# The head of the last feed-forward stage: attention steps behind each gate half and each up half, instead of in pairs behind both

## Chip, core and metric

One Trainium2 chip, one of its cores. The time of a kernel is device microseconds (us) from start to end of one execution. The kernel before takes 408.97 us as the median of three runs (408.11 to 408.98).

## The reference

Two gated transformer blocks on x of 4 batches x 256 tokens x 256 features. Only the second block matters here: attention with 32 heads of 8 features, then a feed-forward layer with 2:4 sparsity. Each is added to x through a tanh gate.

```python
def _L1_xattn_ref(Q, K, V, attention_mask, w_q, w_k, w_v, w_o, b_o):
    ...
    attn = jax.nn.softmax(scores, axis=-1)
    out = jnp.einsum('bnghm,bmgd->bnghd', attn, v).reshape(B, S, D)
    return out @ w_o.T + b_o

def _L1_ffn_ref(x, w_gate, w_up, w_down):
    ...
    h = jax.nn.silu(jnp.einsum('bsh,hi->bsi', x, w_gate)) * jnp.einsum('bsh,hi->bsi', x, w_up)
    h_sparse = _sparsify_2to4(h)       # of each four neighbours the two largest magnitudes stay
    return jnp.einsum('bsi,ih->bsh', h_sparse, w_down)

x = x + jnp.tanh(g_xattn[1]) * _L1_xattn_ref(_layernorm(x, axis=-1), ctx_2048, ctx_2048, ...)
x = x + jnp.tanh(g_ffn[1]) * _L1_ffn_ref(_layernorm(x, axis=-1), ...)
```

## The kernel before

The program is written out engine by engine; each engine runs its own list in the order in which the Python loops emit it, and semaphores tie the lists together. There is no scheduler. Results of TensorE (PE) go to eight banks. `acquire(pe, stage, i, kind)` takes the next bank of a kind in turn and lets PE wait until the reader of what the bank held last has let go of it (`_taken`). In the last stage the gate and up products use kind "wide", banks 0 to 5; all small transposes use kind "turn1", which is one bank, bank 6; the attention's output projection uses "tok1", bank 7.

The 1024 tokens are 8 tiles of 128; a unit is 4 tiles (512 tokens). When the last batch's attention weights have been multiplied with the values, three things are left, and they are mixed:

- The feed-forward layer. One `gate_up(g, j)` is two products of 128 hidden features x 512 tokens, the gate half "fg" and the up half "fu", each of 2 accumulating matmuls over the 256 features (the trace shows a float32 matmul as two instructions, so 4 for each half and 8 for a `gate_up`). There are 16, i = 0 to 15: g = 0, 1 on tokens 0 to 511, g = 2, 3 on tokens 512 to 1023. ScalarE (ACT) takes fg with a Silu (L930) into one of two silu buffers; VectorE (DVE) multiplies fu by it (L1279) and so frees both. ACT then writes the magnitude (L924); DVE, four products later, decides which two of four stay (`sparsify`, four steps for each g, compares L1240 to L1244 first). After i = 15 PE runs the down products: 8 tiles of 16 matmul instructions each; tiles 0 to 3 need `hs_made` 8 and tiles 4 to 7 `hs_made` 16, which DVE counts in `sparsify`.
- `finish(3, n)`, n = 0 to 11, the last batch's attention output: for each of the two tiles six steps. Steps 0 to 3: PE transposes a quarter of the values ("avT", two instructions, L452, bank 6); DVE divides by the softmax sum in two operations, reciprocal (L1176) and multiply into `att` (L1178), and the second frees the bank. Step 4: PE transposes `att` (L242, bank 6) once all four quarters are there, ACT copies it into `actT` (L892). Step 5: PE multiplies by w_o ("res2", 4 instructions, bank 7) after that copy; DVE adds to x (L985) and takes the statistics for the layer norm (L945, L947); GpSimd (POOL) makes the reciprocal deviation `rstd` (L663, L667).
- The layer norm of the tiles 4 to 7: DVE writes `xn` (L957), PE transposes it (`ln_turn`, L236, bank 6), ACT copies into xT (L746). `LATE_NORM_STEPS` = (3, 4, 6, 7) puts the four PE turns behind the gate_ups 3, 4, 6 and 7, and DVE's norms behind its multiplies 2, 3, 5 and 6. The first product on tokens 512 to 1023 (gate_up 8) waits for all eight turns.

The head is the loop over n = 0 to 7 below in PE's list: `gate_up(n)`, then `finish(3, 2n)` and `finish(3, 2n+1)` for n up to 5, then a `ln_turn` where there is one. ACT and DVE walk their own loops over the same i in the same pattern.

Of the kernel before, what the change touches and what calls it, by code (L numbers as in the profile page):

```python
# [7 lines left out]
P = 128  # L8
BATCH, SEQ, DIM = 4, 256, 256
TOKENS = BATCH * SEQ  # L10
TILES = TOKENS // P
KT = DIM // P
# [28 lines left out]
def build_program(nc, a, out):  # L41
# [6 lines left out]
    with ctx:  # L48
        def sb(name, shape, dt=F32):
            return ctx.enter_context(nc.sbuf_tensor(name, shape, dt))  # L50
# [3 lines left out]
        def sem(name):  # L54
            if name not in sems:
                sems[name] = ctx.enter_context(nc.semaphore(name))
            return sems[name]
# [16 lines left out]
        f_gate = f_flat[:, 0:KT * FFN_I].rearrange("p (t n) -> p t n", t=KT)  # L74
        f_up = f_flat[:, KT * FFN_I:2 * KT * FFN_I].rearrange("p (t n) -> p t n", t=KT)
# [22 lines left out]
        xT = sb("xT", [P, KT, TOKENS])  # L98
# [82 lines left out]
        def acquire(pe, stage, i, kind):  # L181

            n = turns.get(kind, 0)
            turns[kind] = n + 1
            bank = KINDS[kind][n % len(KINDS[kind])]
            if bank in occupant:
                before, m = occupant[bank]
                pe.wait_ge(sem(before + "_taken"), m + 1)
            occupant[bank] = (stage, i)
            fills[stage, i] = banks[bank][:, :]  # L190
            return fills[stage, i]

        def filled(eng, stage, i):

            eng.wait_ge(sem(stage + "_ready"), i + 1)
            return fills[stage, i]

        def ready(ins, stage):
            ins.then_inc(sem(stage + "_ready"), 1)

        def taken(ins, stage):
            ins.then_inc(sem(stage + "_taken"), 1)
# [11 lines left out]
        def tile_cols(k):  # L214
            return slice(k * P, (k + 1) * P)
# [11 lines left out]
        def _(pe):  # L227
            def mm(dst, lhsT, rhs, first, last):
                return pe.matmul(dst, lhsT, rhs, start=first, stop=last)  # L229

            def ln_turn(layer, k, kind="turn"):
                dst = acquire(pe, f"ln{layer}", k, kind)
                pe.wait_ge(sem(f"xn{layer}"), k + 1)
                src = xn1[:, HALF_ORDER[k], :] if layer == 1 else xn[:, k % 2, :]
                for t in range(KT):
                    ins = pe.transpose(dst[:, tile_cols(t)], src[:, tile_cols(t)], ident[:, :])  # L236
                ready(ins, f"ln{layer}")

            def turn_pair(stage, i, src, kind):
                dst = acquire(pe, stage, i, kind)  # L240
                for t in range(KT):
                    ins = pe.transpose(dst[:, tile_cols(t)], src[:, tile_cols(t)], ident[:, :])  # L242
                ready(ins, stage)
# [6 lines left out]
            for i in range(4):  # L250
                h, u = divmod(i, UNITS)
                dst = acquire(pe, "rq", i, "main")
                pe.wait_ge(sem("ln0_taken"), UNIT_TILES * (u + 1))
                ready(mm(dst, wh[:, h, :], xT[:, h, u * UNIT:(u + 1) * UNIT], True, True), "rq")
            for i in range(4):
# [3 lines left out]
                dst = acquire(pe, "rk", i, "main")  # L259
                ready(mm(dst, wh[:, h, :], ctxT[:, h, u * UNIT:(u + 1) * UNIT], True, True), "rk")  # L260

            for h in range(RET_HEADS):
                dst = acquire(pe, "rs", h, "main")
                pe.wait_ge(sem("rk_taken"), 2 * h + 2)
                for t in range(2):
                    for b in range(BATCH):
                        at = b * SEQ + t * P
                        ins = mm(dst[:, 2 * P * t:2 * P * t + SEQ - t * P], kT0[:, h, at:at + P],
                                 qT0[:, h, at:(b + 1) * SEQ], b == 0, b == BATCH - 1)
                ready(ins, "rs")  # L270

            for k in range(TILES):
                dst = acquire(pe, "rv", k, "main")
                for h in range(RET_HEADS):
                    ins = mm(dst[:, h * P:(h + 1) * P], ctxT[:, h, tile_cols(k)], wh[:, h, :], True, True)
# [10 lines left out]
            for i in range(4):  # L286
# [3 lines left out]
                dst = acquire(pe, "ro", i, "main")  # L290
                pe.wait_ge(sem("a_made"), 2 * h + 2)
                for t in range(2):
                    ins = mm(dst, amat[:, h, t * SEQ + st * P:t * SEQ + st * P + P], v0[:, t, h, :], t == 0, t == 1)
# [40 lines left out]
            dst = acquire(pe, "rank", 0, "main")[:, 0:(TILES + 1) * EXPERTS].rearrange("p (k e) -> p k e", e=EXPERTS)  # L334
            pe.matmul(dst[:, 0:TILES, :], tri[:, 0, :], onehot16[:, :, :], start=True, stop=False, skip_group_check=True)
            for k in range(TILES):
                later = TILES - k
                ins = pe.matmul(dst[:, k + 1:TILES + 1, :], tri[:, 1, :],
                                onehot16[:, k, :].unsqueeze(1).to_broadcast([P, later, EXPERTS]),
                                start=False, stop=(k == TILES - 1), skip_group_check=True)  # L340
# [101 lines left out]
            def finish(b, n):  # L442

                nt, c = divmod(n, 6)
                i = 2 * b + nt
                if c < PER_GROUP:
                    f = 4 * i + c
                    dst = acquire(pe, "avT", f, "turn1")
                    if c == 0:
                        pe.wait_ge(sem("av_taken"), 4 * b + 2 + nt + 1)  # L450
                    for q in range(HALVES):
                        ins = pe.transpose(dst[:, tile_cols(q)], avT[nt][:, q, c * P:(c + 1) * P], ident[:, :])  # L452
                    ready(ins, "avT")
                elif c == PER_GROUP:
                    pe.wait_ge(sem("avT_taken"), 4 * i + 4)
                    turn_pair("atT", i, att[:, i % 2, :], "turn1")
                else:
                    dst = acquire(pe, "res2", i, "tok1")[:, 0:DIM]
                    pe.wait_ge(sem("atT_taken"), i + 1)
                    for t in range(KT):  # L460
                        ins = mm(dst, actT[:, i % 2, t, :], wo1[:, t, :], t == 0, t == KT - 1)
                    ready(ins, "res2")
# [81 lines left out]
                            scores(b + 2, n)  # L544


            def gate_up(g, j):
                u, blk = divmod(g, FFN_BLOCKS)
                us = slice(u * UNIT, (u + 1) * UNIT)
                c = j * 2 * P + blk * P  # L550
                for stage, w in (("fg", f_gate), ("fu", f_up)):
                    dst = acquire(pe, stage, 4 * g + j, "wide")
                    for t in range(KT):
                        ins = mm(dst, w[:, t, c:c + P], xT[:, t, us], t == 0, t == KT - 1)
                    ready(ins, stage)

            def down(k, kind):
                u, c = k // UNIT_TILES, (k % UNIT_TILES) * P
# [5 lines left out]
            pe.wait_ge(sem("ln3_taken"), UNIT_TILES)  # L564
            loaded(pe, "f", 3)
            for n in range(8):
                gate_up(n // 4, n % 4)
                for c in range(2 * n, min(2 * n + 2, 12)):
                    finish(BATCH - 1, c)
                if n in LATE_NORM_STEPS:  # L570
                    ln_turn(3, UNIT_TILES + LATE_NORM_STEPS.index(n), "turn1")
            pe.wait_ge(sem("ln3_taken"), TILES)
            for j in range(4):
                gate_up(2, j)
            for j in range(4):
                gate_up(3, j)
# [363 lines left out]
        def _(dve):  # L940
# [225 lines left out]
            def finish(b, n):  # L1166
                nt, c = divmod(n, 6)
                i = 2 * b + nt
                if c == 0 and i >= 2:
                    dve.wait_ge(sem("atT_ready"), i - 1)  # L1170
                if c < PER_GROUP:

                    o = att[:, i % 2, :].rearrange("p (q j h d) -> p h q j d", q=HALVES, j=QUADS, h=PER_GROUP)
                    f = 4 * i + c
                    src = filled(dve, "avT", f)[:, 0:2 * P].rearrange("p (q j r) -> p q j r", q=HALVES, j=QUADS)
                    dve.reciprocal(rden[:, f % 2, :, :], src[:, :, :, HD]).then_inc(sem("rden_made"), 1)  # L1176
                    dve.wait_ge(sem("rden_made"), f + 1)
                    taken(dve.tensor_tensor(out=o[:, c, :, :, :], in0=src[:, :, :, 0:HD],  # L1178
                                            in1=rden[:, f % 2, :, :].unsqueeze(3).to_broadcast([P, HALVES, QUADS, HD]),
                                            op=ALU.mult), "avT")  # L1180
                elif c > PER_GROUP:
                    dve.wait_ge(sem("bias_added"), i + 1)
                    residual("res2", i, 1)
                    dve.wait_ge(sem("res2_taken"), i + 1)
                    stat(3, i, x_sb[:, i, :])
# [87 lines left out]
            for g in range(FFN_BLOCKS * UNITS):  # L1273
                for j in range(4):
                    i = 4 * g + j
                    u, blk = divmod(g, FFN_BLOCKS)
                    src = filled(dve, "fu", i)
                    dve.wait_ge(sem("fg_taken"), i + 1)
                    taken(dve.tensor_tensor(out=hs[u][:, 4 * blk + j, :], in0=src, in1=silu[:, i % 2, :], op=ALU.mult), "fu")  # L1279
                    for c in range(2 * i, min(2 * i + 2, 12)):  # L1280
                        finish(BATCH - 1, c)
                    if i + 1 in LATE_NORM_STEPS:
                        norm(3, UNIT_TILES + LATE_NORM_STEPS.index(i + 1))
                    if g >= 1:
                        sparsify(g - 1, j)
# [101 lines left out]
```

## Time and profile before

| | |
|---|---|
| median of three runs | 408.97 us |
| the profiled execution's own time | 409.77 us |
| its span | 407.7 us |
| PE busy in the span | 343.9 us (84%) |
| DVE, ACT, POOL busy | 214.6, 160.1, 98.2 us |
| head of the last stage (gate_up 0 to 7) | 308.9 to 349.7 us |
| gate_up 8 to 15, then the down products | 349.7 to 405.1 us |

An engine's busy time is the sum of its instructions; matmuls are pipelined, so their lengths overlap and the distance between starts says more than a length does. The idle time in brackets behind an instruction group of the timeline is what the engine stood still ahead of it, with the instruction that released it.

### The profile page before, as it was taken

How to read it: one execution, taken by the hardware profiler on the slowest of the kernel's cores; microseconds unless marked ns; L12 is line 12 of the kernel's file. 1: busy time of each engine (PE TensorE's matmuls, PEld its weight loads, DVE VectorE, ACT ScalarE, POOL GpSimd, SP SyncE). 2: the span in 40 equal slices, each digit the busy share in tenths (PEclk: the TensorE clock that was granted, in tenths of full speed). 3: DMA queues.
4: the chain of work that ended last, by engine and by line, in shares of the span. 5: the costliest groups of instructions: out<-in, count | busy, mean ns of one | idle time of the engine just before them, and what ended most of it. 6: DMA issues, size and time to landing. Idle time of an engine off the chain costs nothing.

```text
span 407.7 us, 4563 instructions
## 1 busy us (share of the span) xinstructions
PE 343.9 (84%) x1477; PEld 206.9 (51%) x1477; DVE 214.6 (53%) x509; ACT 160.1 (39%) x336; POOL 98.2 (24%) x148
## 2 busy tenths in 40 slices
PE   2999785519999848989799989979889879999997
PEld 1485564406665526545454555444443434444886
DVE  5134985601232248879446934881241338679921
ACT  2443221204333123145873875477873223333000
POOL 7102543430000346301340442054450001000000
PEclk9999998558999656999999999998999999999999
DMA  7995000143111115400000000000000000000011
GB/s 214 382 424 110 1 13 2 45 151 115 54 39 53 39 47 172 195 6 0 9 0 2 0 6 2 0 2 8 0 2 0 0 2 0 0 0 2 13 51 39
DMA packets 13879, 22.40 MB, mean 55 GB/s; under 512 B 2033, under 2 KB 11249, under 8 KB 13042
## 3 DMA queue, kind: packets, MB, share of 16 engines
q1 hardware_dynamic: 13090, 20.03, 14.4%
q0 software_dynamic: 768, 2.10, 1.6%
q8 instruction: 12, 0.20, 0.2%
q14 instruction: 9, 0.07, 0.1%
HBM read 15.83 MB, written 6.03 MB: 54 GB/s over the span
## 4 chain that ended last, share of the span: by engine, by line
PE 58%; DVE 19%; ACT 8%; issue 7%; POOL 4%; DMA 3%; SPq 0%; DVEq 0%; ACTq 0%; POOLq 0%
PE bank L229 43%; DVE mx L1150 8%; PE bank L438 5%; ACT region L874 5%; PE bank L406 3%; DVE stats L945 2%; POOL x_sorted L691 2%; PE bank L409 2%; PE bank L242 1%; POOL rstd L667 1%; DVE x_sb L985 1%; ACT qst L825 1%; PE bank L452 1%; DMA x_sb<-in_x_dram 1%; PE bank L486 1%
## 5 line engine op out<-in xcount | busy, mean ns | idle before, releaser
L1150 DVE TENSOR_REDUCE mx<-bank 128x2 f32<-128x512 f32 (+1 forms) x96 | 59.8, 684 | 14.0 <-PE bank L409 14.0
L874 ACT ACTIVATE region<-bank,padcol 128x512 f32<-128x512 f32 x96 | 60.8, 701 | 12.6 <-PE bank L229 11.6
L729 POOL TENSOR_SCALAR_AFFINE_SELECT region<-region 128x1024 f32<-128x1024 f32 x32 | 35.0, 1094 | 94.6 <-ACT region L874 94.3
L229 PE MATMUL bank<-xT,e_gu 128*128 128x512 f32 x128 | 56.6, 594 | 0.5 <-ACT xT L746 0.5
L229 PE MATMUL bank<-qst,kblk 128*128 128x512 f32 x96 | 46.1, 507 | 1.6 <-ACT region L874 0.7
L406 PE MATMUL bank<-kblk,qst 128*128 128x512 f32 x96 | 43.3, 475 | 1.6 <-DVE mx L1150 0.9
L229 PEld LDWEIGHTS bank<-xT,e_gu 128*128 128x128 f32 x128 | 23.8, 190 | 28.0 <-issue 27.1
L663 POOL TENSOR_SCALAR veps<-mv 128x1 f32<-128x1 f32 x40 | 11.3, 283 | 80.5 <-DVE mv L947 80.1
L409 PE MATMUL bank<-causb,identb 128*128 128x256 bf16 (+1 forms) x96 | 30.6, 319 | 0.0
L746 ACT ACTIVATE xT<-bank 128x256 f32<-128x256 f32 x32 | 12.4, 386 | 44.1 <-PE bank L236 43.9
L229 PE MATMUL bank<-e_down,region 128*128 128x256 f32 x128 | 27.8, 379 | 0.0
L985 DVE SCALAR_TENSOR_TENSOR x_sb<-bank,tg,x_sb 128x256 f32<-128x256 f32 x24 | 11.6, 482 | 29.2 <-PE bank L229 28.9
L236 PE MATMUL bank<-ident,xn 128*128 128x128 f32 x48 | 12.2, 350 | 17.2 <-DVE xn L957 15.2
L229 PEld LDWEIGHTS bank<-e_down,region 128*128 128x128 f32 x128 | 24.3, 190 | 3.7 <-issue 0.5
L406 PEld LDWEIGHTS bank<-kblk,qst 128*128 128x128 f32 x96 | 18.3, 190 | 13.2 <-DVE mx L1150 9.3
L667 POOL TENSOR_TENSOR rstd<-veps,power 128x1 f32<-128x1 f32 x40 | 24.2, 604 | 3.3
L1122 DVE TENSOR_TENSOR sact<-bank,silu 128x176 f32<-128x176 f32 x15 | 5.1, 342 | 37.6 <-ACT silu L840 37.6
L1279 DVE TENSOR_TENSOR region<-bank,silu 128x512 f32<-128x512 f32 x16 | 11.0, 690 | 26.0 <-PE bank L229 26.0
L229 PEld LDWEIGHTS bank<-qst,kblk 128*128 128x128 f32 x96 | 18.7, 201 | 9.1 <-ACT region L874 7.3
L930 ACT ACTIVATE silu<-bank 128x512 f32<-128x512 f32 x16 | 9.6, 597 | 33.5 <-PE bank L229 33.5
L438 PE MATMUL bank<-region,vaug 128*32 128x512 f32 x192 | 22.7, 597 | 0.0
L229 PE MATMUL bank<-e_gu,sT 128*128 x60 | 21.8, 488 | 0.3 <-ACT sT L834 0.3
(155 smaller groups left out, 557.0 us busy)
## 6 DMA issues: line engine op xcount, KB each, us to landing
e_gu<-in_e_gu_dram SPq DMA_DIRECT2D x2, 1408.0 KB, 12.6
x_sorted<-zero SPq DMA_DIRECT2D x1, 1920.0 KB, 10.3
y_sorted<-region SPq DMA_DIRECT2D x15, 128.0 KB, 1.7
x_sb<-in_x_dram SPq DMA_DIRECT2D x4, 256.0 KB, 4.0
ctxT<-in_ctxT_dram SPq DMA_DIRECT2D x2, 512.0 KB, 7.6
e_down<-in_e_down_dram SPq DMA_DIRECT2D x1, 1024.0 KB, 13.6
region<-x_sorted SPq DMA_DIRECT2D x1, 1024.0 KB, 7.4
e_gu<-in_f_gate_dram SPq DMA_DIRECT2D x1, 1024.0 KB, 4.8
```

Of the source, the lines that this page charges most:

```text
L229: return pe.matmul(dst, lhsT, rhs, start=first, stop=last)
L236: ins = pe.transpose(dst[:, tile_cols(t)], src[:, tile_cols(t)], ident[:, :])
L406: pe.matmul(dst, qst[:, s, q, hg, tile_cols(nt)], kblk[s][q][:, quads, 0:(nt + 1) * P], start=True, stop=False, skip_group_check=True)
L409: ready(pe.matmul(diagonal, identb[:, :], causb[:, 0:diagonal.shape[1], :], start=False, stop=True, skip_group_check=True), "sa")
L438: ins = pe.matmul(dst[32 * j:32 * j + 32, :], vaug[:, 2 * b + mt, 4 * q + j, :], rhs, start=(mt == 0), stop=(mt == nt), skip_group_check=True)
L663: pool.tensor_scalar(veps[:, layer, k:k + 1], mv[:, layer, k, 1:2], eps, None, ALU.add)\
L667: pool.tensor_tensor(out=rstd[:, layer, k:k + 1], in0=veps[:, layer, k:k + 1], in1=power[:, :], op=ALU.pow).then_inc(sem(f"rstd{layer}"), 1)
L729: pool.affine_select(out=block, in_=block, compare_op=ALU.is_ge, fill=0.0, base=0, pattern=[[0, 2], [0, PER_GROUP], [1, P]], channel_multi ...
L746: taken(act.activation(xT[:, :, tile_cols(tile)], src[:, 0:DIM].rearrange("p (t n) -> p t n", t=KT), ACT.Copy), f"ln{layer}")
L874: taken(act.activation(dst, src.rearrange("p (h n) -> p h n", n=SEQ - mt * P), ACT.Exp, bias=padcol[:, key:key + 1], scale=float(HD) ** -0 ...
L985: dve.scalar_tensor_tensor(out=x_sb[:, tile, :], in0=filled(dve, stage, k)[:, 0:DIM], scalar=tg[:, g:g + 1], in1=x_sb[:, tile, :], op0=ALU ...
L1150: taken(dve.reduce_max(mx[:, b % 2, nt, quads, q, hg], src, AX), "sa")
```

## The change

The halves become a function of their own, `half_piece`. In PE's list `finish(3, 2n)` now stands between the gate half and the up half, and `finish(3, 2n+1)` behind the up half. In DVE's list `finish(3, 2i)` moves ahead of the multiply of fu, `finish(3, 2i+1)` stays behind it. The lists of ACT, POOL and SyncE, and the order in which banks are acquired within each kind, stay as they were. No instruction is added or removed.

```diff
@@ -544,15 +544,18 @@
                             scores(b + 2, n)
 
 
-            def gate_up(g, j):
+            def half_piece(stage, w, g, j):
                 u, blk = divmod(g, FFN_BLOCKS)
                 us = slice(u * UNIT, (u + 1) * UNIT)
                 c = j * 2 * P + blk * P
-                for stage, w in (("fg", f_gate), ("fu", f_up)):
-                    dst = acquire(pe, stage, 4 * g + j, "wide")
-                    for t in range(KT):
-                        ins = mm(dst, w[:, t, c:c + P], xT[:, t, us], t == 0, t == KT - 1)
-                    ready(ins, stage)
+                dst = acquire(pe, stage, 4 * g + j, "wide")
+                for t in range(KT):
+                    ins = mm(dst, w[:, t, c:c + P], xT[:, t, us], t == 0, t == KT - 1)
+                ready(ins, stage)
+
+            def gate_up(g, j):
+                half_piece("fg", f_gate, g, j)
+                half_piece("fu", f_up, g, j)
 
             def down(k, kind):
                 u, c = k // UNIT_TILES, (k % UNIT_TILES) * P
@@ -564,9 +567,12 @@
             pe.wait_ge(sem("ln3_taken"), UNIT_TILES)
             loaded(pe, "f", 3)
             for n in range(8):
-                gate_up(n // 4, n % 4)
-                for c in range(2 * n, min(2 * n + 2, 12)):
-                    finish(BATCH - 1, c)
+                half_piece("fg", f_gate, n // 4, n % 4)
+                if 2 * n < 12:
+                    finish(BATCH - 1, 2 * n)
+                half_piece("fu", f_up, n // 4, n % 4)
+                if 2 * n < 12:
+                    finish(BATCH - 1, 2 * n + 1)
                 if n in LATE_NORM_STEPS:
                     ln_turn(3, UNIT_TILES + LATE_NORM_STEPS.index(n), "turn1")
             pe.wait_ge(sem("ln3_taken"), TILES)
@@ -1274,11 +1280,13 @@
                 for j in range(4):
                     i = 4 * g + j
                     u, blk = divmod(g, FFN_BLOCKS)
+                    if 2 * i < 12:
+                        finish(BATCH - 1, 2 * i)
                     src = filled(dve, "fu", i)
                     dve.wait_ge(sem("fg_taken"), i + 1)
                     taken(dve.tensor_tensor(out=hs[u][:, 4 * blk + j, :], in0=src, in1=silu[:, i % 2, :], op=ALU.mult), "fu")
-                    for c in range(2 * i, min(2 * i + 2, 12)):
-                        finish(BATCH - 1, c)
+                    if 2 * i < 12:
+                        finish(BATCH - 1, 2 * i + 1)
                     if i + 1 in LATE_NORM_STEPS:
                         norm(3, UNIT_TILES + LATE_NORM_STEPS.index(i + 1))
                     if g >= 1:
```

PE's list from the head's first gate half on, before (a number behind "bank" is the bank; L229 are products, with `xT,e_gu` the gate and up halves in turn and `wo1,actT` the output projection, L452 the quarter transposes, L242 the `att` transpose):

```order
L229 MATMUL bank2<-xT,e_gu 128x512 x2
L229 MATMUL bank3<-xT,e_gu 128x512 x2
L452 MATMUL bank6<-ident,prod 128x128 x4
L229 MATMUL bank4<-xT,e_gu 128x512 x2
L229 MATMUL bank5<-xT,e_gu 128x512 x2
L452 MATMUL bank6<-ident,prod 128x128 x4
L229 MATMUL bank0<-xT,e_gu 128x512 x2
L229 MATMUL bank1<-xT,e_gu 128x512 x2
L242 MATMUL bank6<-ident,att 128x128 x2
L229 MATMUL bank7<-wo1,actT 128x256 x2
```

The same place now:

```order
L229 MATMUL bank2<-xT,e_gu 128x512 x2
L452 MATMUL bank6<-ident,prod 128x128 x2
L229 MATMUL bank3<-xT,e_gu 128x512 x2
L452 MATMUL bank6<-ident,prod 128x128 x2
L229 MATMUL bank4<-xT,e_gu 128x512 x2
L452 MATMUL bank6<-ident,prod 128x128 x2
L229 MATMUL bank5<-xT,e_gu 128x512 x2
L452 MATMUL bank6<-ident,prod 128x128 x2
L229 MATMUL bank0<-xT,e_gu 128x512 x2
L242 MATMUL bank6<-ident,att 128x128 x2
L229 MATMUL bank1<-xT,e_gu 128x512 x2
L229 MATMUL bank7<-wo1,actT 128x256 x2
```

Two fills of bank 6 that stood back to back (x4) now have half a gate_up between them, and so have the `att` transpose and the projection that needs it. At n = 3 and 4 a layer-norm transpose follows. Before:

```order
L229 MATMUL bank2<-xT,e_gu 128x512 x2
L229 MATMUL bank3<-xT,e_gu 128x512 x2
L452 MATMUL bank6<-ident,amat 128x128 x4
L236 MATMUL bank6<-ident,xn 128x128 x2
L229 MATMUL bank4<-xT,e_gu 128x512 x2
```

And now:

```order
L229 MATMUL bank2<-xT,e_gu 128x512 x2
L452 MATMUL bank6<-ident,amat 128x128 x2
L229 MATMUL bank3<-xT,e_gu 128x512 x2
L452 MATMUL bank6<-ident,amat 128x128 x2
L236 MATMUL bank6<-ident,xn 128x128 x2
L229 MATMUL bank4<-xT,e_gu 128x512 x2
```

Of three fills of bank 6 in a row, two are left in a row. DVE's list for n = 0, before (L1279 is the multiply of fu, of bank 3 here):

```order
L1279 TENSOR_TENSOR region<-bank3,silu 128x512
L1176 RECIPROCAL rden<-bank6 128x8
L1178 TENSOR_TENSOR att<-bank6,rden 128x8x8
L1176 RECIPROCAL rden<-bank6 128x8
L1178 TENSOR_TENSOR att<-bank6,rden 128x8x8
```

And now (the lines are those of the changed file, six or eight higher):

```order
L1182 RECIPROCAL rden<-bank6 128x8
L1184 TENSOR_TENSOR att<-bank6,rden 128x8x8
L1287 TENSOR_TENSOR region<-bank3,silu 128x512
L1182 RECIPROCAL rden<-bank6 128x8
L1184 TENSOR_TENSOR att<-bank6,rden 128x8x8
```

The first of the two quarter steps has moved ahead of the multiply; the second stands behind it as before.

## Rows read from the trace of the kernel before

**Rows 1.** The page: the span, PE and its granted clock in 40 slices.

```profile
span 407.7 us, 4563 instructions
...
PE   2999785519999848989799989979889879999997
...
PEclk9999998558999656999999999998999999999999
```

**Rows 2.** Stretches: busy time (instructions) of PE, PEld, DVE, ACT, POOL; PEclk.

```profile
308.90:349.70 40.80, 34.34 (x104) 16.35 (x100) 19.25 (x47) 12.10 (x23) 2.04 (x4) 1.00 0.00 0
349.70:405.00 55.30, 55.28 (x192) 36.41 (x192) 35.24 (x60) 10.04 (x18) 0.00 (x0) 1.00 0.05 17
```

**Rows 3.** The chain of waits, 309 to 350 us: start, length, what.

```profile
312.66 0.24 DVE region L1279
...
313.27 0.21 DVE rden L1176
...
313.50 0.24 DVE att L1178
...
313.78 0.44 PE bank L452 x2
...
322.94 0.39 ACT actT L892
...
323.46 4.55 PE bank L229 x12
```

**Rows 4.** Timeline of PE through the head: start, length, what, idle before.

```profile
308.92 3.70 PE L229 MATMUL bank<-xT,e_gu 128*128 128x512 f32 x8
312.46 0.38 PE L452 MATMUL bank<-ident,prod 128*128 128x128 f32 x2
313.78 0.44 PE L452 MATMUL bank<-ident,prod 128*128 128x128 f32 x2 [0.94 <-DVE att L1178]
314.05 3.60 PE L229 MATMUL bank<-xT,e_gu 128*128 128x512 f32 x8
...
319.08 3.60 PE L229 MATMUL bank<-xT,e_gu 128*128 128x512 f32 x8
...
324.40 3.60 PE L229 MATMUL bank<-xT,e_gu 128*128 128x512 f32 x8
...
330.43 3.60 PE L229 MATMUL bank<-xT,e_gu 128*128 128x512 f32 x8
...
336.45 3.60 PE L229 MATMUL bank<-xT,e_gu 128*128 128x512 f32 x8
...
341.77 3.60 PE L229 MATMUL bank<-xT,e_gu 128*128 128x512 f32 x8
...
345.43 3.60 PE L229 MATMUL bank<-xT,e_gu 128*128 128x512 f32 x8
...
349.71 2.84 PE L229 MATMUL bank<-xT,e_gu 128*128 128x512 f32 x6 [0.47 <-ACT xT L746]
```

**Rows 5.** The page: the Silu of the gate halves.

```profile
L930 ACT ACTIVATE silu<-bank 128x512 f32<-128x512 f32 x16 | 9.6, 597 | 33.5 <-PE bank L229 33.5
```

**Rows 6.** Timeline of DVE: compare, multiply 5, two norms, last sparsify step.

```profile
337.59 1.76 DVE L1240 TENSOR_TENSOR ctxT<-region 128x1536 bf16<-128x1536 f32 x1 [1.46 <-ACT region L924]
...
341.00 0.69 DVE L1279 TENSOR_TENSOR region<-bank,silu 128x512 f32<-128x512 f32 x1
...
343.12 0.40 DVE L957 TENSOR_SCALAR xn<-x_sb,mv,rstd 128x256 f32<-128x256 f32 x1
...
346.77 0.41 DVE L957 TENSOR_SCALAR xn<-x_sb,mv,rstd 128x256 f32<-128x256 f32 x1
...
388.25 1.28 DVE L1270 SCALAR_TENSOR_TENSOR region<-amat,region 128x512 f32<-128x512 bf16 x2
```

**Rows 7.** Line 667 from 300 to 350 us: shortest, median, longest ns; starts.

```profile
L667 POOL TENSOR_TENSOR rstd<-veps,power x4: 567/570/863, 305.1 to 343.7; 128x1 f32<-128x1 f32 x4
```

**Rows 8.** Stretches, as rows 2: one with a lower granted clock.

```profile
132.50:142.70 10.20, 8.78 (x28) 5.50 (x26) 2.46 (x5) 1.58 (x7) 3.33 (x4) 0.68 0.11 39
```

## The prediction

> **What bounds the kernel now.** I read the page first, then the stretches, then the chain of waits and PE's timeline in the head. The page shows PE busy in nearly every slice of the second half, at full granted clock from slice 32 on [rows 1]. The two stretches separate the last stage: from 349.7 us to the end PE is busy 55.28 of 55.30 us, so nothing but PE's own work counts there; in the head it is busy 34.34 of 40.80 us, at a granted clock of 1.00, which is its upper level, 2.4 GHz [rows 2]. Whatever PE stands still in the head is therefore paid in full at the end, and the head is the place to price. DVE is busy 19.25 us and ACT 12.10 us of it: neither is short of time, PE waits for single operations of theirs.
>
> The chain shows which. At the end of gate_up 0 PE has put the first quarter into bank 6 and needs the same bank for the second. DVE holds it up with three operations in a row: the multiply of fu from 312.66, the reciprocal at 313.27, the multiply into `att` at 313.50, and PE goes on at 313.78 [rows 3]. From 312.46 to 313.78 is 1.32 us for one fill and one release [rows 4]. The other kind of wait is that of the projection for ACT's copy of the `att` transpose (322.94, and PE on at 323.46) [rows 3].
>
> **Sizing the waits.** I take the price of PE's pure work from the tail, where it never waits: 55.28 us for 64 instructions of 512 columns and 128 of 256, which is 0.432 us for one of 512 and 0.216 for one of 256 [rows 2]. A gate_up is 8 x 0.432 = 3.46 us, a half 1.73, a projection 4 x 0.216 = 0.86. gate_up 6 with one transpose pair and no wait takes 345.43 - 341.77 = 3.66 us [rows 4], so a pair costs 0.20. Now each step of the head, start to next start [rows 4], less its pure work:
>
> - n = 0: 314.05 - 308.92 = 5.13, less 3.46 and 2 pairs = 1.27 (0.10 of it is start-up: 308.92 to 312.46 is 3.54 where others take about 3.44)
> - n = 1: 5.03 - 3.86 = 1.17
> - n = 2: 5.32 - 3.46 - 0.20 - 0.86 = 0.80
> - n = 3: 6.03 - 3.46 - 3 pairs = 1.97
> - n = 4: 6.02 - 4.06 = 1.96
> - n = 5: 5.32 - 4.52 = 0.80
>
> Together 7.97 us. Ahead of gate_up 8 there is one more wait, 0.47 us for ACT's copy into xT [rows 4].
>
> **What the change does to each.** Two uses of bank 6 within a gate_up are now a pair and a half apart, 0.20 + 1.73 = 1.93 us, where the worst release in the trace, the one with a multiply of fu ahead of it, takes 1.32. The release of the first step no longer has the multiply in front, that of the second still has, and behind it PE has the next gate half to run: 0.6 us to spare in both. So the 1.17 of n = 0 and of n = 1 go.
>
> At n = 2 and 5 the projection now comes 1.93 us after the start of the `att` transpose, where it came 0.94 after it, waiting. But the gate half's Silu is now ready with the transpose and stands ahead of the copy in ACT's list: 0.60 us [rows 5], which puts the projection at 0.94 + 0.60 = 1.54 at worst. 0.4 us to spare: both 0.80 go. The cover is the up half; without it the price would be 0.80 + 0.60 each.
>
> At n = 3 and 4 three uses of bank 6 become two in a row, `finish(2n+1)` and the layer-norm transpose. DVE's release of the last quarter still has the multiply of fu ahead, so this wait is the 1.17 of n = 1; what goes is 1.97 - 1.17 = 0.80 and 1.96 - 1.17 = 0.79. Its next fill of bank 6 comes a gate half after ACT's copy began, so nothing is left over from there.
>
> Sum of what goes: 1.17 + 1.17 + 0.80 + 0.80 + 0.79 + 0.80 = 5.53 us. No instruction is added. PE's switch between shapes costs nothing new: n = 6 has the same products and a pair at 3.66 us [rows 4].
>
> **What is late next.** DVE has the same work in less time, so I carried its list through. By the steps above gate_up 5 starts about 4.65 us earlier than its 336.45 (n = 0, 1 and 2, 3, 4: 1.17 + 1.17 + 0.80 + 0.80 + 0.79 = 4.73, less rounding): 331.8. The compares began 1.14 us after that start and the multiply 5 behind them 4.55 after it [rows 6]; they hang on that layer-norm turn and ACT, so they move with it: multiply 5 at 336.35. The norms of tiles 6 and 7 follow it by 2.12 and 5.77 us [rows 6]: 338.5 and 342.1, done 0.4 later. PE reaches the turns at 331.8 + 1.73 + 0.20 + 1.73 + 0.86 + 3.46 = 339.8 and, with 0.20 + 3.46 more, 343.4. Both norms are there 0.9 us before. The wait ahead of gate_up 8 stays as it is. In the tail `hs_made` 16 is complete at 389.53 [rows 6] and needed when the last 64 of PE's instructions begin, about 405.1 - 64 x 0.216 = 391.3: 1.7 us to spare, and DVE's last multiply hangs on PE, so both move together.
>
> One rule bears on the norm of tile 7, which needs `rstd` from POOL. The row: L667 takes 0.57 us but once 0.86, the last, begun at 343.7, while DVE runs `sparsify` operations with two inputs in SBUF [rows 7]. The Trainium skill, "SBUF — State Buffer", section "Who interferes with whom", says that a VectorE instruction with two SBUF inputs and a GpSimd instruction that reads SBUF exclude each other for a whole instruction. The trace agrees as far as 0.29 us goes. By the row `rstd` is ready 2 us before the norm. By the rule at its harshest POOL would come on only behind all seven `sparsify` operations and the norm would start some tenths late, still inside the 0.9; it adds nothing to the sum and a little to rival 2.
>
> **The number.** 409.77 - 5.53 = 404.24 us for the profiled execution. That execution lies 0.80 above the median of the three runs, 408.97, so I expect a median of 403.5 us, a gain of 1.35%. Bounds of the uncertain terms: what is left at n = 3 and 4 may be 1.1 to 1.3 each, the spare 0.4 to 0.9 us may be used up once, and the median of before may itself be off by 0.5: 402.7 to 404.6 for the likeliest case.
>
> **Rivals.**
>
> 1. *The projection's wait stays.* ACT's copy stands behind a Silu that now becomes ready at the same moment. For it: the order in ACT's list is unchanged. Against it: 0.4 us to spare by the rows. If the two projection waits stay at 0.80 the gain is 3.9 us: 405.1 us. Chance 0.07.
> 2. *DVE becomes the late one.* Multiply 5 stands behind 3.4 us of compares, and the norms of tiles 6 and 7 behind it. If that chain came 2 us later than I have it, 1.1 us would be lost at the two last turns: 404.6 us. Were DVE's tail chain not to move at all with PE, only its 1.7 us spare would remain as gain: 407.3 us. For it: DVE is the busiest reader (35.24 of 55.30 us in the tail); against it: it idles in between. Chance 0.07, nearly all at the first price.
> 3. *The granted clock falls in the head (slower).* The finer mix of transposes and products, or another alignment, leaves part of the head at the lower level, 1.2 GHz. The trace has a stretch with PE busy 8.78 of 10.2 us at a mean grant of only 0.68 [rows 8]. The head's 32.2 us of pure work (40.80 - 7.97 - about 0.6) at 0.68 would cost 32.2 x (1/0.68 - 1) = 15.2 us: 418.7 us. It decides from a mean grant of 0.85 down, where 32.2 x (1/0.85 - 1) = 5.7 eats the gain. Against it: the head had 1.00 with more standing still than now, and the tail has 1.00 with none [rows 2]. Chance 0.02.
> 4. *It does not do what it says:* some wait I don't see stands in front of each half, for instance for a gate or up bank that is given back late, and the wait only moves. The six banks of that kind are acquired in the same order, three gate_ups apart, and no such wait shows now. 408 to 409 us. Chance 0.04.
>
> The forecast has 0.80. What a measurement of this kernel can tell from no change is about 0.2%, 0.8 us. Slower by more than that: rival 3 and half a hundredth or so of the unforeseen, 0.03. Within it: most of rival 4, 0.03. Faster: 0.94. The range, 402.6 to 405.4, takes in the likeliest case with rival 1 and the first price of rival 2.
>
> **What would show it.** In the changed profile: the L452 pairs with no idle before them; the projection with none; two idles of about 0.94 us ahead of L236 (behind the `att` multiply, 1.3 us after the pair before), and the 0.47 ahead of gate_up 8. gate_up 0 to 7 should last about 35.3 us where they lasted 40.8, and the tail still 55.3. Wrong would be: idle ahead of L452 pairs or the projection (1), ahead of the last two L236 (2), a PEclk under 1.00 in the head (3), idle ahead of gate or up halves (4).

## The result and the profile after

| | before | changed |
|---|---|---|
| median of 6 runs, us | 409.15 (408.11 to 410.38) | 403.04 (402.38 to 405.15) |
| profiled execution's own time, us | 409.77 | 402.70 |
| span, us | 407.7 | 400.6 |
| head (first gate half to gate_up 8), us | 40.79 | 35.33 |

The ratio is 0.9858, with a 95% interval from 0.9832 to 0.9884: a gain of 1.2 to 1.7%, where 1.35% was forecast. The median forecast was 403.5 us, the measured one is 403.04. One of the six changed executions, the one of 405.15 us, had a mean granted clock of 0.928 over its span where the other five had 0.936; it was not profiled, so no row shows in which stage its clock was lower.

PE's timeline of the changed kernel through the head (start, length, what, and in brackets the idle time ahead; the products are still L229, the turns L236) answers [rows 4]:

```profile
307.26 1.98 PE L229 MATMUL bank<-xT,e_gu 128*128 128x512 f32 x4
309.08 0.38 PE L452 MATMUL bank<-ident,prod 128*128 128x128 f32 x2
309.30 1.88 PE L229 MATMUL bank<-xT,e_gu 128*128 128x512 f32 x4
311.02 0.38 PE L452 MATMUL bank<-ident,prod 128*128 128x128 f32 x2
311.24 1.88 PE L229 MATMUL bank<-xT,e_gu 128*128 128x512 f32 x4
...
316.83 0.38 PE L242 MATMUL bank<-ident,att 128*128 128x128 f32 x2
...
318.77 1.03 PE L229 MATMUL bank<-wo,actT 128*128 128x256 f32 x4
...
323.29 0.38 PE L452 MATMUL bank<-ident,amat 128*128 128x128 f32 x2
324.61 0.44 PE L236 MATMUL bank<-ident,xn 128*128 128x128 f32 x2 [0.94 <-DVE att L1184]
324.88 1.88 PE L229 MATMUL bank<-xT,e_gu 128*128 128x512 f32 x4
...
329.86 0.44 PE L236 MATMUL bank<-ident,xn 128*128 128x128 f32 x2 [0.94 <-DVE att L1184]
330.13 1.88 PE L229 MATMUL bank<-xT,e_gu 128*128 128x512 f32 x4
...
338.08 0.38 PE L236 MATMUL bank<-ident,xn 128*128 128x128 f32 x2
...
341.74 0.38 PE L236 MATMUL bank<-ident,xn 128*128 128x128 f32 x2
342.59 9.71 PE L229 MATMUL bank<-xT,e_gu 128*128 128x512 f32 x22 [0.47 <-ACT xT L752]
```

No idle stands ahead of any L452 pair or of the projection at 318.77; the two idles of 0.94 ahead of the layer-norm turns of n = 3 and 4 and the 0.47 ahead of gate_up 8 are all that is left. 342.59 - 307.26 = 35.33 us. The two stretches, in the columns of [rows 2]:

```profile
307.26:342.59 35.33, 32.99 (x104) 16.17 (x100) 19.15 (x47) 11.90 (x23) 2.04 (x4) 1.00 0.00 0
342.59:398.00 55.41, 55.36 (x192) 36.40 (x192) 35.20 (x61) 10.03 (x18) 0.00 (x0) 1.00 0.05 17
```

The head keeps its granted clock of 1.00, and PE still doesn't wait in the tail. From gate_up 8 to the end of the span it is 58.0 us in both kernels (407.7 - 349.71 and 400.6 - 342.59): nothing is given back.

The two spans differ by 7.1 us and the heads by 5.46 only. The other 1.66 us lie ahead of the head, which begins at 308.92 before and at 307.26 now. That is not the change: in the ten profiled executions of this text the head begins between 306.77 and 309.36, and all their kernels have the same lists up to there. The length of the head is therefore what the experiments below are read by; it was the same to 0.01 us in both profiled executions of pe_only below.

### The profile page after: what moved, and what is told of

Same layout as the page of the kernel before. It is cut to its first block, busy times and chain, and to the rows that moved or that the text cites. A ratio compares the mean times of both kernels' runs of the same rounds, so it can differ in the third digit from the quotient of the medians.

```text
span 400.6 us, 4557 instructions
## 1 busy us (share of the span) xinstructions
PE 340.5 (85%) x1471; PEld 205.7 (51%) x1477; DVE 214.3 (54%) x509; ACT 160.0 (40%) x336; POOL 98.4 (25%) x148
## 3 DMA queue, kind: packets, MB, share of 16 engines
HBM read 15.83 MB, written 6.03 MB: 55 GB/s over the span
## 4 chain that ended last, share of the span: by engine, by line
PE 57%; DVE 20%; ACT 8%; issue 7%; POOL 4%; DMA 3%; another core or an unknown queue 1%; SPq 0%; DVEq 0%; ACTq 0%; POOLq 0%
PE bank L229 43%; DVE mx L1156 9%; ACT region L880 5%; PE bank L438 5%; PE bank L406 3%; DVE stats L951 2%; POOL x_sorted L697 2%; POOL rstd L673 2%; PE bank L242 1%; DVE x_sb L991 1%; PE bank L409 1%; DMA x_sb<-in_x_dram 1%; PE bank L452 1%; PE bank L486 1%; PE bank L236 1%
## 5 line engine op out<-in xcount | busy, mean ns | idle before, releaser
L229 PE MATMUL bank<-xT,e_gu 128*128 128x512 f32 x128 | 57.6, 594 | 0.5 <-ACT xT L752 0.5
L229 PE MATMUL bank<-qst,kblk 128*128 128x512 f32 x96 | 46.0, 506 | 1.6 <-ACT region L880 0.7
L229 PEld LDWEIGHTS bank<-xT,e_gu 128*128 128x128 f32 x128 | 23.3, 190 | 25.1 <-issue 24.3
L409 PE MATMUL bank<-causb,identb 128*128 128x256 bf16 (+1 forms) x90 | 28.3, 314 | 0.0
L229 PE MATMUL bank<-e_down,region 128*128 128x256 f32 x128 | 27.8, 379 | 0.0
L236 PE MATMUL bank<-ident,xn 128*128 128x128 f32 x48 | 12.2, 349 | 18.2 <-DVE xn L963 15.5
L991 DVE SCALAR_TENSOR_TENSOR x_sb<-bank,tg,x_sb 128x256 f32<-128x256 f32 x24 | 11.5, 480 | 27.8 <-PE bank L229 27.5
L229 PEld LDWEIGHTS bank<-e_down,region 128*128 128x128 f32 x128 | 24.3, 190 | 3.7 <-issue 0.5
L229 PEld LDWEIGHTS bank<-qst,kblk 128*128 128x128 f32 x96 | 18.8, 202 | 9.0 <-ACT region L880 7.2
L229 PE MATMUL bank<-e_gu,sT 128*128 x60 | 21.6, 484 | 0.3 <-ACT sT L840 0.3
L229 PE MATMUL bank<-e_down,sT 128*128 (+1 forms) x60 | 19.6, 426 | 1.4 <-ACT sT L861 1.4
```

Of the source, the lines that this page charges most:

```text
L409: ready(pe.matmul(diagonal, identb[:, :], causb[:, 0:diagonal.shape[1], :], start=False, stop=True, skip_group_check=True), "sa")
L991: dve.scalar_tensor_tensor(out=x_sb[:, tile, :], in0=filled(dve, stage, k)[:, 0:DIM], scalar=tg[:, g:g + 1], in1=x_sb[:, tile, :], op0=ALU ...
```

## The experiments

Each is a small change of the kernel before or of the changed kernel; turn_mid and norm_early build on ln_bank7. "Head" is, in each trace, from the first gate half to the first half of gate_up 8. The medians are of 4 to 10 executions (pe_only_again: one), the ratios against executions of the kernel before run alongside, whose medians were 409.36 us for pe_only, dve_only, two_banks and ln_bank7, 409.69 us for copy_late, turn_mid, norm_early and pe_only_again, and 409.15 us for the changed kernel.

| kernel | head, us | median, us | ratio (95%) |
|---|---|---|---|
| before | 40.79 | 409.15 | |
| changed | 35.33 | 403.04 | 0.9858 (0.9832 to 0.9884) |
| pe_only | 41.77 | 410.17 | 1.0013 (0.9998 to 1.0028) |
| pe_only_again | 41.77 | 411.20 | |
| dve_only | 39.42 | 408.04 | 0.9965 (0.9945 to 0.9985) |
| two_banks | 36.49 | 404.85 | 0.9890 (0.9866 to 0.9913) |
| copy_late | 35.33 | 403.71 | 0.9852 (0.9833 to 0.9871) |
| ln_bank7 | 33.02 | 402.24 | 0.9807 (0.9783 to 0.9832) |
| turn_mid | 32.96 | 401.79 | 0.9810 (0.9795 to 0.9825) |
| norm_early | 32.40 | 401.26 | 0.9794 (0.9779 to 0.9810) |

**Only PE's list (pe_only).** The changed kernel with DVE's list put back:

```diff
-                    if 2 * i < 12:
-                        finish(BATCH - 1, 2 * i)
                     src = filled(dve, "fu", i)
...
-                    if 2 * i < 12:
-                        finish(BATCH - 1, 2 * i + 1)
+                    for c in range(2 * i, min(2 * i + 2, 12)):
+                        finish(BATCH - 1, c)
```

> PE's list as in the changed kernel (halves apart), DVE's list as before (both steps of finish behind the multiply of fu). My theory: at n = 0, 1, 3, 4 PE's wait is for DVE's release of bank 6 behind the multiply, so splitting PE's list alone only moves it from in front of the second pair's old place to its new one: it stays at about 1.1 us each at n = 0 and 1, and two waits each at n = 3 and 4; only the two projection waits at n = 2 and 5 (0.80 each) go. Head 40.8 - 1.6 = 39.2 us, about 407.5 us in all. Rival (distance alone does it: half a gate_up between two fills of bank 6 hides the release wherever DVE has the multiply): head near the 35.3 us of the changed kernel, about 403 us.

Measured: no gain; the head is 0.98 us longer. PE's timeline:

```profile
310.15 1.88 PE L229 MATMUL bank<-xT,e_gu 128*128 128x512 f32 x4
313.19 0.44 PE L452 MATMUL bank<-ident,prod 128*128 128x128 f32 x2 [1.16 <-DVE att L1184]
...
322.37 1.03 PE L229 MATMUL bank<-wo,actT 128*128 128x256 f32 x4
...
329.20 0.64 PE L236 MATMUL bank<-ident,xn 128*128 128x128 f32 x2 [0.56 <-DVE att L1184]
329.64 3.41 PE L229 MATMUL bank<-xT,e_gu 128*128 128x512 f32 x4
332.89 0.38 PE L452 MATMUL bank<-ident,amat 128*128 128x128 f32 x2
```

And DVE's, at n = 0:

```profile
312.07 0.69 DVE L1285 TENSOR_TENSOR region<-bank,silu 128x512 f32<-128x512 f32 x1 [7.91 <-PE bank L229]
312.68 0.20 DVE L1182 RECIPROCAL rden<-bank 128x8 f32<-128x8 f32 x1
```

The rival is out: distance alone does not help. The first quarter is in bank 6 early, but DVE comes to it only behind the multiply, which waits for the up half; so the second quarter still waits for multiply, reciprocal and multiply into `att`, 1.16 us of idle against 0.94 before. From the up half's end to the second quarter it is 1.32 us in both kernels; before, the first pair's 0.22 us lay inside that time, now they are paid besides it. The projection waits are gone, as expected. Step by step, from PE's starts, the head of pe_only lasts 5.36, 5.25, 4.52, 6.40, 7.77 and 4.52 us for n = 0 to 5, against 5.13, 5.03, 5.32, 6.03, 6.02 and 5.32 [rows 4]. So my 39.2 us was wrong twice. The waits behind the multiply are about 0.22 us longer each, 0.88 in all. And at n = 4 there is something new, the gate half that starts at 329.64 and takes 3.25 us where others take 1.72. The stretches, in the columns of [rows 2]:

```profile
323.20:328.20 5.00, 3.85 (x11) 1.51 (x10) 2.50 (x8) 0.60 (x1) 0.87 (x2) 1.00 0.00 0
328.20:329.60 1.40, 0.83 (x4) 0.60 (x5) 0.75 (x3) 0.00 (x0) 0.00 (x0) 0.89 0.00 0
329.60:332.90 3.30, 3.30 (x7) 1.28 (x6) 0.00 (x0) 0.90 (x2) 0.00 (x0) 0.53 0.00 0
```

The granted clock was 0.53 in this stretch, in effect its lower level of 1.2 GHz (finer stretches have 0.50 from 329.3 to 332.5 us). Ahead of it PE had waited 1.16 us, turned one pair, waited 0.56 more and begun the next pair. The layer-norm turn ahead of the gate half is slow too, 0.44 us from start to start where it is 0.27 otherwise, so the lower clock costs 1.53 + 0.17 = 1.70 us. That is rival 3 of the prediction, in the wrong kernel. To see whether it was chance I ran the same kernel once more.

> The kernel of pe_only once more, to see whether the lower granted clock (0.53 from 329.6 to 332.9 us, behind waits of 1.16 and 0.56 us) comes again. If it belongs to this order of waits: the gate half after the layer-norm turn of n = 3 or 4 takes about 3.3 us instead of 1.7 again, head 41 to 42 us. If it was a chance of that execution: head 40.2 us (the step lengths of pe_only without the 1.53 us of the slow half).

It came again in nearly the same place, and the head lasted 41.77 us again; the one execution took 411.20 us. Its stretches:

```profile
325.00:330.00 5.00, 3.71 (x12) 1.40 (x10) 2.26 (x8) 0.60 (x1) 0.87 (x2) 1.00 0.00 0
330.00:335.00 5.00, 4.58 (x10) 2.33 (x11) 0.66 (x3) 1.50 (x3) 0.00 (x0) 0.66 0.02 3
```

Here the gate half takes 3.01 us, and the pair and the up half behind it lose 0.20 each: 1.7 us again. So in both profiled executions the lower clock came at n = 4 and cost 1.7 us. The other executions were not profiled; their mean granted clocks fit it, 0.929 or 0.933 in all eleven executions of this kernel against 0.933 or 0.937 in the 31 of the kernel before run alongside (3.3 us at 0.53 lower a mean over 408 us by 0.004). Without the lower clock the head would be 41.77 - 1.70 = 40.07 us, 0.72 under before: 1.60 less for the projections, 0.88 more for the bank.

**Only DVE's list (dve_only).** The kernel before with `finish(3, 2i)` ahead of DVE's multiply:

```diff
+                    if 2 * i < 12:
+                        finish(BATCH - 1, 2 * i)
                     src = filled(dve, "fu", i)
...
-                    for c in range(2 * i, min(2 * i + 2, 12)):
-                        finish(BATCH - 1, c)
+                    if 2 * i < 12:
+                        finish(BATCH - 1, 2 * i + 1)
```

> DVE's list as in the changed kernel (first step of finish ahead of the multiply of fu), PE's list as before (both steps behind both halves). My theory: the wait between the two pairs falls from 1.32 to about 0.99 us start to start (a release without the multiply in front), 0.33 us less at each of n = 0, 1, 3, 4; at n = 3 and 4 the layer-norm turn then meets the multiply and gives 0.33 or more back; n = 2 and 5 unchanged. Head about 40.0 us (39.5 to 40.8), in all 408.0 to 409. Rival (DVE's order is what mattered): more than 2 us gained.

Measured: head 39.42, 1.37 us shorter. PE and DVE at n = 3:

```profile
325.07 0.38 PE L452 MATMUL bank<-ident,amat 128*128 128x128 f32 x2
326.08 0.44 PE L452 MATMUL bank<-ident,amat 128*128 128x128 f32 x2 [0.63 <-DVE att L1178]
327.08 0.44 PE L236 MATMUL bank<-ident,xn 128*128 128x128 f32 x2 [0.56 <-DVE att L1178]
```

```profile
325.80 0.22 DVE L1178 TENSOR_TENSOR att<-bank,rden 128x64 f32<-128x64 f32 x1
325.94 0.68 DVE L1281 TENSOR_TENSOR region<-bank,silu 128x512 f32<-128x512 f32 x1
326.56 0.21 DVE L1176 RECIPROCAL rden<-bank 128x8 f32<-128x8 f32 x1
```

The head is just under the 39.5 to 40.8 that I expected, the median of 408.04 within the 408 to 409. The first release is 0.3 to 0.4 us earlier, as expected, at all four places. What I expected to be given back at n = 3 and 4 is not: the multiply runs while PE fills the bank for the second time, and the layer-norm turn waits 0.56 as before. DVE's order alone is worth 1.4 us; PE's alone would be worth 0.7 and gave nothing, with the lower clock; both together bring 5.46. The parts don't add up: only with both lists changed is the first quarter's release early and a half there to cover it.

**Another bank instead (two_banks).** The kernel before, but the last batch's quarters take banks 6 and 7 in turn:

```diff
-                    dst = acquire(pe, "avT", f, "turn1")
+                    dst = acquire(pe, "avT", f, "last" if b == BATCH - 1 else "turn1")
```

> The kernel before with one thing else: the last batch's quarter transposes take banks 6 and 7 in turn instead of bank 6 alone. My theory (the waits at n = 0, 1, 3, 4 are for the bank and for nothing else): both waits of 1.17 at n = 0 and 1 go, at n = 3 and 4 the layer-norm turn on bank 6 still waits about 0.9 for the release of the pair before last, so 1.97 falls to about 0.9 each; the projection waits of 0.80 at n = 2 and 5 stay. Head 40.8 - 2.3 - 2.1 = 36.4 us, in all about 404.7 us. Rival (the waits are for att or another product of the same DVE operations): no change, 409 us.

Measured: head 36.49 us against 36.4 expected, median 404.85 against 404.7. PE's timeline:

```profile
310.31 0.60 PE L452 MATMUL bank<-ident,prod 128*128 128x128 f32 x4
310.75 3.60 PE L229 MATMUL bank<-xT,e_gu 128*128 128x512 f32 x8
...
319.00 1.10 PE L229 MATMUL bank<-wo,actT 128*128 128x256 f32 x4 [0.56 <-ACT actT L892]
...
323.38 0.60 PE L452 MATMUL bank<-ident,amat 128*128 128x128 f32 x4
324.70 0.44 PE L236 MATMUL bank<-ident,xn 128*128 128x128 f32 x2 [0.72 <-DVE att L1178]
```

Both pairs run on without a gap; with no instruction moved, the second bank alone brings 4.3 of the 5.5 us. The waits between the pairs at n = 0, 1, 3 and 4 were for the bank and nothing else; the layer-norm turn still waits for bank 6 (0.72 us of idle), and the waits of the projection, untouched here, are the other kind. What the changed kernel has over this one, 36.49 - 35.33 = 1.16 us, is the 1.60 of the projections less 0.22 at each of n = 3 and 4, where the layer-norm turn waits longer in the changed kernel.

**How much the up half covers (copy_late).** The changed kernel, ACT's list at i = 2 and 5:

```diff
+                if i in (2, 5):
+                    magnitude(i - 1)
                 for c in range(2 * i, min(2 * i + 2, 12)):
                     finish(BATCH - 1, c)
...
-                if i >= 1:
+                if i >= 1 and i not in (2, 5):
                     magnitude(i - 1)
```

> The changed kernel, with ACT's magnitude operation (0.62 us) put ahead of its copy of the att transpose at i = 2 and 5. It asks how much the up half really covers. In the changed kernel the copy began 0.70 us after the att transpose and PE came to the projection 1.94 us after it; with the 0.52 from a copy's start to PE's next start that would leave 0.72 us to spare, where my prediction had 0.4. Measured spare right: the copy comes about 0.5 to 0.6 later, still no idle ahead of the projection, head 35.3 us, 403 us. If the 0.4 of the prediction were right: 0.1 to 0.2 us idle at both, head 35.6. If the cover were no cover (rival: the projection's order in ACT's list is what counts): 1.2 us more.

Measured: the head is the same 35.33 us to the hundredth. ACT's and PE's rows at n = 2:

```profile
318.22 0.60 ACT L936 ACTIVATE silu<-bank 128x512 f32<-128x512 f32 x1 [2.76 <-PE bank L229]
318.71 0.62 ACT L930 ACTIVATE region<-region 128x512 f32<-128x512 f32 x1
319.23 0.38 ACT L898 ACTIVATE actT<-bank 128x256 f32<-128x256 f32 x1
```

```profile
318.02 0.38 PE L242 MATMUL bank<-ident,att 128*128 128x128 f32 x2
318.24 1.88 PE L229 MATMUL bank<-xT,e_gu 128*128 128x512 f32 x4
319.96 1.03 PE L229 MATMUL bank<-wo,actT 128*128 128x256 f32 x4
```

The copy starts 1.21 us after the transpose, and 0.52 later PE could go on, at 319.75; it comes at 319.96. Two operations ahead of the copy still fit, with 0.2 us left. The copy came 0.51 us later at no cost, so the 0.4 of the prediction is out; 0.51 + 0.21 is the 0.72 read from the rows.

**The waits that are left (ln_bank7).** The changed kernel with the last four turns on bank 7:

```diff
-                    ln_turn(3, UNIT_TILES + LATE_NORM_STEPS.index(n), "turn1")
+                    ln_turn(3, UNIT_TILES + LATE_NORM_STEPS.index(n), "tok1")
```

> The changed kernel with the last four layer-norm turns on bank 7 (kind tok1) instead of bank 6. Bank 7 is free at n = 3 and 4, its last reader there being the residual of n = 2. My theory (what is left at n = 3 and 4 is only the wait for bank 6 behind the multiply): both idles of 0.94 us ahead of L236 go and 1.1 us of head with each; head 35.3 - 2.2 = 33.1 us, in all 400.8 us, 0.55% under the changed kernel. The 0.47 ahead of gate_up 8 stays. Rival (DVE becomes late: its compares and the norms of tiles 6 and 7 do not come forward with PE): idles of up to 1 us ahead of the turns of n = 6 and 7, head 34 to 35 us, 402 to 403 us.

Measured: head 33.02 us, 2.31 shorter, where 33.1 was expected. The median, 402.24, is 1.4 us above my figure of 400.8, which was the changed kernel's median less 2.2 and left the spread ahead of the head out: the five executions here lie between 400.74 and 402.56, and in the profiled one the head begins at 309.36, 2.1 us later than in the changed kernel's. The ratio falls by 0.5% from the changed kernel's as expected, though the two intervals touch; what shows the gain is the head. PE's timeline at n = 3:

```profile
325.39 0.38 PE L452 MATMUL bank<-ident,amat 128*128 128x128 f32 x2
325.61 0.38 PE L236 MATMUL bank<-ident,xn 128*128 128x128 f32 x2
```

**The last wait, in two steps (turn_mid, norm_early).** turn_mid is ln_bank7 with the turn of tile 7 moved from behind gate_up 7 to between its halves; norm_early also moves DVE's norm of tile 7 ahead of multiply 6. The lines that take the two out of their old places are left out here.

```diff
                 half_piece("fg", f_gate, n // 4, n % 4)
...
+                if n == 7:
+                    ln_turn(3, TILES - 1, "tok1")
                 half_piece("fu", f_up, n // 4, n % 4)
...
+                    if i == 6:                      # norm_early alone
+                        norm(3, TILES - 1)
                     src = filled(dve, "fu", i)
```

> On top of ln_bank7: the last layer-norm turn (tile 7) between the halves of gate_up 7 instead of behind them, DVE's list unchanged. The wait ahead of gate_up 8 (0.47 idle, 0.63 in all) is for ACT's copy of that turn. Theory: PE reaches the turn 1.72 us earlier and now waits there for DVE's norm 7, which is bound by DVE's own chain (compares, multiply 5, sparsify, multiply 6): that norm ended at about 340.5 in the changed kernel, where the gate half ended at 340.0, so some 0.3 to 0.5 us of wait there, none ahead of gate_up 8: head 32.7 to 33.0 us. Rival (PE alone decides, DVE has time): head 32.4.

> turn_mid, and DVE's norm 7 ahead of its multiply 6 (0.60 us earlier). Theory: the norm is then ready about when the gate half of gate_up 7 ends, no wait at the turn or at most 0.1, none ahead of gate_up 8, multiply 6 0.3 later without a reader who waits for it: head 32.4 us, 0.6 under ln_bank7, 1.5 to 1.7% under the kernel before by the tail's unchanged 58.0 us; total about 401.6 us if the stretch ahead of the head is the mean of the executions so far (307.9). Rival (rstd of tile 7 is late, since POOL meets the sparsify operations): the norm stalls DVE, multiply 6 and 7 come late, head 33 us or more.

PE's timeline at the turn, first of turn_mid, then of norm_early:

```profile
339.83 0.41 PE L236 MATMUL bank<-ident,xn 128*128 128x128 f32 x2 [0.37 <-DVE xn L965]
340.08 16.47 PE L229 MATMUL bank<-xT,e_gu 128*128 128x512 f32 x38
```

```profile
338.42 0.38 PE L236 MATMUL bank<-ident,xn 128*128 128x128 f32 x2
338.64 17.76 PE L229 MATMUL bank<-xT,e_gu 128*128 128x512 f32 x41
```

In turn_mid the wait has become one for DVE's norm, 0.37 us, and the wait ahead of gate_up 8 is gone; in norm_early there is none at all. (Gate_up 8 follows the up half without a break, so I take its start as 1.73 us after the start of that half: 341.81 and 340.37.) The heads are 32.96 and 32.40 us, as the two theories had them. norm_early has the lowest median of these kernels: 401.26 us, 2.1% under before. Its ratio's interval does not meet that of the changed kernel; between ln_bank7, turn_mid and norm_early the intervals overlap, and only the heads tell them apart.

## Why the prediction was right

- *PE's idle time in the head is paid in full.* Right: 5.46 us shorter there, and the last stage's remainder unchanged at 58.0 us. That the whole comes within 0.5 us of the forecast is in part luck, since the time ahead of the head alone varies by 2.6 us.
- *The sizes.* 7.97 us of waits in the head, of which 5.53 were to go: 5.46 went. In the changed kernel n = 0 lasts 311.24 - 307.26 = 3.98 us; less 3.46 and two pairs that leaves 0.12, the start-up. n = 4 lasts 330.13 - 324.88 = 5.25 us; less 4.06 that leaves 1.19, where the prediction had 1.17.
- *Why the bank waits go.* Shown: two_banks takes the waits between the pairs away with no order changed, pe_only brings them back with DVE's order. The prediction reasoned that the multiply no longer stands ahead of the first release and that a gate half covers the second; pe_only and dve_only show that it takes both.
- *The projection.* Right that both waits go; the term of its sum that was mis-sized is the spare, 0.4 for 0.72 us. I had put the Silu's full 0.60 ahead of the copy [rows 5]. In the trace it begins 0.20 after the `att` transpose starts, since it hangs on the gate half alone, and a next operation of ACT starts 0.1 before the last one's end (rows of copy_late: 318.22, 0.60, 318.71). So the copy comes only 0.28 us later than before (0.70 after the transpose, 0.42 then). ACT's rows of the changed kernel, where the transpose starts at 316.83:

```profile
317.03 0.60 ACT L936 ACTIVATE silu<-bank 128x512 f32<-128x512 f32 x1 [2.76 <-PE bank L229]
317.53 0.38 ACT L898 ACTIVATE actT<-bank 128x256 f32<-128x256 f32 x1
```

- *DVE behind PE.* Multiply 5 was to start 4.55 us after gate_up 5; it did, 334.68 - 330.13. The norms of tiles 6 and 7 were there 1.3 us ahead of PE, not 0.9, since the residual (L991) ahead of norm 6 no longer waits for the projection: it starts 0.60 us after multiply 5, 1.04 before. DVE's rows:

```profile
334.68 0.68 DVE L1287 TENSOR_TENSOR region<-bank,silu 128x512 f32<-128x512 f32 x1
335.28 0.47 DVE L991 SCALAR_TENSOR_TENSOR x_sb<-bank,tg,x_sb 128x256 f32<-128x256 f32 x1
...
336.35 0.40 DVE L963 TENSOR_SCALAR xn<-x_sb,mv,rstd 128x256 f32<-128x256 f32 x1
...
340.00 0.40 DVE L963 TENSOR_SCALAR xn<-x_sb,mv,rstd 128x256 f32<-128x256 f32 x1
```

- *The shared port.* The harshest reading that the prediction gives to the rule it cites from the Trainium skill, POOL only behind all seven `sparsify` operations, is out. `rstd` of tile 7 began at 336.91 and took 0.86 us, ready at 337.77, while those operations ran from 336.66 to 339.48. It took 0.29 us more than most others of its line, as before [rows 7], and no run here shows what the 0.29 are:

```profile
336.91 0.86 POOL L673 TENSOR_TENSOR rstd<-veps,power 128x1 f32<-128x1 f32 x1
```

- *The rivals.* 1, 2 and 4 are out by the idle times above. 3, the clock, did not come in the head of the changed kernel's profiled execution but did in pe_only, at 1.7 us and not at the 15.2 us of its price. The argument against it, that the head kept 1.00 with more standing still than now, does not hold as a rule: pe_only stands still less than the kernel before, 7.97 - 0.72 = 7.25 us of waits in the head, and its clock fell.

Still open: why the clock falls at n = 4 of pe_only and not in the kernel before, whose waits there are 0.94 and 0.56 us against 1.16 and 0.56. The changed kernel has the same PE list as pe_only, with those waits of 1.16 us gone, and its head kept 1.00, so PE's order alone does not bring it; no run has waits of 1.16 us in PE's order of before.

## What to carry to other kernels

When PE waits for a buffer, look at what stands ahead of the release in the reader's list, not only at the distance between PE's two uses: of the 5.46 us that both lists gave, DVE's alone gave a quarter, and PE's alone nothing (0.7 us, lost again to the lower clock). A second buffer, where one lies idle, does most of the same in one line, and what is left of such waits can be taken in turn until the reader itself is the late one. Judge changes of a few microseconds by the stretch that they touch: here the time ahead of it varied by 2.6 us between executions, half the gain.

## What the hardware showed that I had not expected

Another pattern of short waits can bring a lower clock that costs more than the waits it saves. In pe_only PE's waits of 1.16 us (where before they were 0.94) were followed at n = 4 by some 3.3 us at the lower granted clock, in both profiled executions at nearly the same place: 1.7 us on top, which ate the 0.7 us that the order would otherwise have gained. In the profiled execution of every other kernel the head stayed at 1.00, in the kernel before too, whose waits in the head add up to more. So their sum does not tell, nor does PE's order alone, which the changed kernel shares; whether it is the longer single waits or where they fall is not shown.
